# Routing each image by itself inside the causal attention, and POOL's selections of the last image ahead of its scatters

## What is computed

```python
t = t + _L3_attn_ref(_ln_t(t), L3_attn_w_qkv, L3_attn_w_out)   # causal attention, 8 heads of 16, per image
t = t + _L3_ffn_ref(_ln_t(t), W_router, W1, b1, W2, b2)        # 8 experts, top 2
# inside _L3_ffn_ref:
logits = x_flat @ W_router
topk_p, topk_i = jax.lax.top_k(softmax(logits), 2)
```

## Time and profile before

| | us |
|---|---|
| median of 3 runs | 1439.09 (1438.96 to 1439.64) |
| the profiled execution's own time | 1437.34 |
| its span, first to last instruction | 1435.5 |
| busy in the span: PE, DVE, ACT, POOL | 1106.5, 844.0, 676.1, 609.9 |

### The profile page before, as it was taken

How to read it: one execution, slowest core, us unless ns; L and a number is a source line. 1 busy time by engine, 2 the same in 40 slices (tenths; PEclk the granted TensorE clock), 3 DMA queues, 4 the chain that set the end, 5 groups by cost and what they waited for, 6 DMA issues and landing times. The chain is left out here.

```text
span 1435.5 us, 31817 instructions
## 1 busy us (share of the span) xinstructions
PE 1106.5 (77%) x9500; PEld 890.7 (62%) x9500; DVE 844.0 (59%) x2747; ACT 676.1 (47%) x1475; POOL 609.9 (42%) x873
## 2 busy tenths in 40 slices
PE   4549785888797967393799999548999984489982
PEld 3339553455465756262699999525667663489981
DVE  5754697663658754652355555356565574567764
ACT  3422473563555544161466666315555641355541
POOL 4600243035655533177134444212246667466660
PEclk9859998999999966597799999859999995699995
DMA  2148001100000005311111111124000001222216
GB/s 73 49 78 120 7 29 40 24 13 13 9 11 1 3 2 240 135 54 52 34 49 48 48 48 46 45 77 163 1 10 24 20 20 41 55 61 59 62 55 178
DMA packets 83095, 75.11 MB, mean 52 GB/s; under 512 B 21808, under 2 KB 75824, under 8 KB 81712
## 3 DMA queue, kind: packets, MB, share of 16 engines
q1 hardware_dynamic: 72880, 53.01, 13.4%
q0 software_dynamic: 9984, 20.53, 4.4%
q10 hardware_dynamic: 128, 0.26, 0.1%
HBM read 44.82 MB, written 29.48 MB: 52 GB/s over the span
## 5 line engine op out<-in xcount | busy, mean ns | idle before, releaser
L1782 POOL DMA_INDIRECT ys_scratch<-m_yout,m_xin x152 | 161.3, 1061 | 208.8 <-DVE m_yout L1884 147.8
L1816 PE MATMUL m_eps_up<-m_ext,m_w_up 128*128 128x128 f32 x1856 | 237.5, 279 | 0.7 <-DVE m_w_up L1863 0.7
L1816 PEld LDWEIGHTS m_eps_up<-m_ext,m_w_up 128*128 128x128 f32 x1856 | 222.5, 194 | 2.9 <-issue 1.2
L1826 PE MATMUL m_eps_y<-m_w_down,m_ht 128*128 128x128 f32 x1216 | 160.5, 275 | 0.6 <-DVE m_ht L1876 0.5
L1826 PEld LDWEIGHTS m_eps_y<-m_w_down,m_ht 128*128 128x128 f32 x1216 | 147.8, 192 | 1.0 <-DVE m_ht L1876 0.7
L1837 ACT ACTIVATE m_w_up<-m_up 128x512 f32 x152 | 95.8, 630 | 102.3 <-PE m_eps_up L1816 48.3
L1297 POOL TENSOR_TENSOR a_z<-a_y,a_peak 128x16 f32<-128x16 f32 (+31 forms) x64 | 67.6, 1057 | 105.7 <-DVE a_peak L1208 94.1
L2326 DVE TENSOR_REDUCE c_peak<-c_ps_s 128x2 f32<-128x256 f32 (+1 forms) x128 | 65.3, 552 | 80.4 <-PE c_ps_s L2617 79.9
L1840 ACT ACTIVATE m_w_down<-m_down 128x512 f32 x152 | 94.4, 621 | 17.4 <-PE m_eps_y L1826 17.2
L2165 POOL TENSOR_SCALAR_AFFINE_SELECT c_e<-c_e 128x256 f32<-128x256 f32 x128 | 49.2, 409 | 123.2 <-ACT c_e L2242 123.1
L1201 DVE SCALAR_TENSOR_TENSOR a_y<-a_y,a_ps_row 128x1 f32<-128x1 f32 (+51 forms) x256 | 72.3, 282 | 38.7 <-POOL a_z L1297 29.5
(11 more groups left out here) (394 smaller groups left out, 2595.2 us busy)
## 6 DMA issues: line engine op xcount, KB each, us to landing
m_xin<-xs_scratch SPq DMA_DIRECT2D x152, 64.5 KB, 1.8
xs_scratch<-empty SPq DMA_DIRECT2D x12, 516.0 KB, 11.0
m_y<-ys_scratch SPq DMA_DIRECT2D x22, 256.0 KB, 5.0
m_up<-in_m_gate SPq DMA_DIRECT2D x2, 2048.0 KB, 7.5
m_up<-in_m_up SPq DMA_DIRECT2D x2, 2048.0 KB, 11.9
m_down<-in_m_down SPq DMA_DIRECT2D x2, 2048.0 KB, 23.7
a_q_in<-q_scratch SPq DMA_DIRECT2D x80, 32.0 KB, 1.7
c_rows<-ys_scratch SPq DMA_DIRECT2D x10, 256.0 KB, 3.6
```

Of the source, the lines that this page charges most:

```text
L1782: pool.indirect_dma_start(ys_dram, bass.IndirectOffsetOnAxis(xin[:, u, C:C + 1].bitcast(U32), 0), yout[:, u, :], None).then_inc(stored[u], 16)
L1816: last = pe.matmul(ps[u % 2][:, k * P:(k + 1) * P], w[:, u % 2, k * P:(k + 1) * P], xt[:, u % 2, :], start=True, stop=True)
L1826: last = pe.matmul(ps_y[u % 2][:, 0:C], ht[:, u % 2, k, :], w_down[:, u % 4, k, :], start=(k == 0), stop=(k == KC - 1))
```

## The change

All lots hold one image. There are 16 passes of choosing and ranking in place of 11, one at every step. `send(b)` is at step `b+6` for every image. At step `B` = 16, POOL runs all the selections of image 15, also that of quarter 3 which stood at step 17, ahead of `invert(13)` and of the scatters; before, four scatters stood ahead of the selection of quarter 2 and four more ahead of that of quarter 3.

```diff
-LAST_PAIR = 10
-LOTS = [(b, 2) for b in range(0, LAST_PAIR, 2)] + [(b, 1) for b in range(LAST_PAIR, B)]
+LOTS = [(b, 1) for b in range(B)]
...
             for i in range(-2, B + 7):
                 before, last_but_one = 0 <= i - 1 < B, 0 <= i - 2 < B
-                if last_but_one:
+                if last_but_one and i <= B:
                     cut_off(i - 2, 3)
                 if before:
                     cut_off(i - 1, 0)
-                if before:
                     cut_off(i - 1, 1)
+                if i == B:
+                    cut_off(i - 1, 2)
+                    cut_off(i - 1, 3)
                 if 0 <= i - 3 < B:
                     invert(i - 3)
-                if 0 <= i - 7 < LAST_PAIR:
-                    send(i - 7, 0, 2)
-                if LAST_PAIR <= i - 6 < B:
+                if 0 <= i - 6 < B:
                     send(i - 6, 0, 2)
-                if before:
+                if before and i < B:
                     cut_off(i - 1, 2)
-                if 0 <= i - 7 < LAST_PAIR:
-                    send(i - 7, 2, 4)
-                if LAST_PAIR <= i - 6 < B:
+                if 0 <= i - 6 < B:
                     send(i - 6, 2, 4)
                 if 0 <= i - 4 < B:
                     copy_rows(i - 4)
```

## The result

| us | before | changed |
|---|---|---|
| median of 20 runs each | 1440.61 (1436.63 to 1442.78) | 1448.85 (1440.90 to 1456.76) |
| ratio, 95% interval | | 1.0052 (1.0039 to 1.0066) |
| the profiled execution's own time | 1437.34 | 1450.59 |
| its span | 1435.5 | 1448.9 |

The change is slower, by 0.5% in the ratio and 8.2 us between the medians. 1441.0 had been forecast and 1444.5 was the top of the range. The changed kernel's runs also lie wider apart: 16 us against 6.

What follows compares the result with a forecast made beforehand. DVE's path between row maxima, plus 7.6 us set by PE, was taken to bound each step. Steps +9.0 and end -7.1 gave +1.9 us, 1441.0 us on the median; range 1438.5 to 1444.5.

Steps and rivals of the forecast that it cites:

- what bounds a step: Steps of the attention: DVE's path from first to third row maximum, plus a constant 7.6 us set by PE.
- Rival 3: Steps 6 to 15: DVE hides the extra choosing passes, path 6.15 us; faster, 1432.5 us; chance 0.07.
- the way: DVE, first to third maximum in steps 6 to 15: 7.00 us each, +9.0 us in total.
- The upper end of 10.0: Top of the steps' cost: 0.1 us more at each of ten steps for PE's wait for the logits.
- the wait for the logits: PE waits for the logits ahead of the rank; 0.1 us more per step, only in the upper end.
- the end: From step 16 to the last padding: earlier selection of quarter 3 lets the padding land 7.1 us earlier.
- the other is 0.5 us: Step 16, clock already halved when the last quarter is weighed: gain 6.6 us instead of 7.1.
- a gain of 5.7 as its lower bound: Block's end: gain is only 5.7 us if POOL's scatters, not the padding, end it.
- the added wait: Step 16: DVE waits in shift_of(13) for invert(13), delaying PE's rank and weighing; weighing 6.6 us earlier, not 8.8.
- Rival 1: Last scatter groups: POOL bounds the end, 0.5 us more per group of four; slower, 1443.3 us; chance 0.17.
- its own sign: Block's end: padding issued well before the last scatter would show POOL as the bound; forecast had the scatter 0.7 us ahead.
- Rival 2: Steps: choosing on DVE loses 0.39 us per step to POOL's selections; slower, 1444.9 us; chance 0.08.

Runs made afterwards that it cites:

- before_2: The kernel before the change, nothing changed, profiled a second time in one run; 1440.39 us.
- e9: Changed kernel with fifteen idle bf16 matmuls of 384 columns at three places of PE's step 16; median 1448.99 us, ratio 1.0071 to before.
- e1_again: Second profile of the changed kernel with POOL's old order back, so only the routing image by image is left; one run, 1452.72 us.
- e1: Changed kernel with POOL's old order back, so only the routing image by image is left; median 1448.38 us, ratio 1.0070 to before.
- e5: Changed kernel with invert(13) moved between POOL's selections of quarters 2 and 3 at step 16; median 1448.13 us, ratio 1.0053 to before.
- e2: Kernel before, pairs kept, only POOL's selections of the last image moved ahead of all scatters of step 16; median 1439.85 us, ratio 1.0017.

## Why the prediction was wrong, point by point

**Right: what bounds a step.** The third maximum has no idle time, the second waits for PE, choosing and slots both stand between, and a step is its way plus 7.6 us. Rival 3 (hidden) did not occur as long as the order stayed. The lengths 14.7 to 14.8 fit the 14.6 that were named.

**A term mis-sized: the way.** It was put at 7.00 us and is 7.18. Of this 0.08 is the rank, 0.66 us for the 0.58 worked out from the earlier trace rows: of its three groups of matmuls the first takes 0.21 until the next starts, and 0.10 had been extrapolated for each added pair. The other 0.10 is the slots: they take 1107.88 - 1106.73 = 1.15 us, hardly less than the 1.21 of two images in the earlier trace rows; the 1.06 of the earlier trace rows stood at another step. The way is paid in ten steps, which makes 1.8 us; step 5 grew by 0.07, and the last 0.2 are spread over steps that were 0.01 to 0.03 longer. So 9.0 became 11.1. The upper end of 10.0 had only the wait for the logits in it.

**The step that failed: the end.** 7.1 us were forecast and 0.7 measured in the profiled execution, 2.4 when executions with the same early fall are compared. The prediction took the last exponential's place behind the maximum from the earlier trace rows as fixed, and weighed the clock only behind it ("the other is 0.5 us"), since it had fallen at 1189 in the one profile at hand. before_2, the same kernel, shows the exponential 4.8 us later. So the first term of the end's sum, the time from which POOL can select, had a spread of 4.8 us that one profile can't show. Before, eight scatters hid it; the change removes the scatters and makes the exponential the start of the chain. The gain counted from it, 8.8 us of which 6.6 were left, belongs to an execution with a late fall, and every profile of the changed kernel has an early one. With an early fall the exponential in before_2 is over at 1191.15 and the selection starts at 1196.77, so only 5.6 us were to be had, of which the weighing got 26.5 - 23.9 = 2.6 and the padding 2.4.

A smaller part of the miss has nothing to do with the exponential's place. The forecast has the padding 30.8 us behind the exponential's end (1223.56 - 7.1 - 1185.65), and it starts 32.4 behind it in all four profiles of the changed kernel. Of these 1.6 us, 0.8 are the rank matmuls at half the clock. The place of the last scatter was right: 34.8 behind the exponential's end by the forecast's 1220.4, 34.9 measured. So 7.1 - 1.6 - 4.8 gives the 0.7 that were measured, and a changed kernel with a late fall would have gained 5.5 us. That is an estimate from these figures, and e9, the changed kernel with idle matmuls and a late fall, bears it out: padding 32.4 and last scatter 34.9 behind the end of its last exponential. The prediction had kept a gain of 5.7 as its lower bound, for the case that POOL's scatters end the block, but went by the padding.

A second error stands beside it: the placement and the single lots were priced as one. The weighing was seen as freed from eight scatters, but the single lots had already taken four of them away. With an early fall, POOL issues the four that remain while it would wait for exponentials anyway, and the added wait and the four scatters put behind the last selection cost more than the placement saves (e1_again). With a late fall the two orders come out nearly even: the loads are 46.2 us behind the last exponential's start in e1's first profile and 45.6 in e9.

**Right: the added wait.** `shift_of(13)`, the logits' copy, `rank_of(11)`, the weighing: this chain stands in the profile word for word. The weighing is 3.8 us behind the exponential's end, for 3.0: the rank matmuls took 1207.31 - 1205.96 = 1.35 us at half the clock and not 0.58.

**Rival 1, POOL.** By its own sign, a last scatter behind the padding, it did not occur: the last scatter starts 2.1 us ahead of the end of SP's padding issue, as it did before, and not 0.7. Its price, 0.5 us more for each group of four, did not come either, since the last scatter is where the forecast had it. But the sign was badly chosen. The loads follow the last scatter wherever the two part (e5 above all), and POOL's queue is full from the last selection on but for the 0.39 us, so POOL was the bound of this end or as good as level with it.

**Rival 2, the port.** It did not occur, for its condition was hardly met. The choosing runs from 1108.56 to the third maximum at 1109.56, and POOL's selections beside it from 1106.76 to 1107.53 and again from 1109.40, so only the choosing's last instruction touches one. The second part of the way was 0.10 us longer than forecast, not 0.39. What the whole choosing would lose beside a selection, no run here shows. What does meet a selection is the slots' L2426, with two SBUF inputs: 0.62 us for its pair in the rows above, beside the first of these selections. At the end of the attention in e2, with POOL at scatters, DVE shows for the same pair:

```profile
1209.80 0.38 DVE L2431 TENSOR_TENSOR n_part<-n_rank,n_pick 128x16 f32<-128x16 f32 x2
```
By the Trainium skill, page "SBUF — State Buffer", section "Who interferes with whom", a DVE instruction with two SBUF inputs and a GpSimd instruction that reads SBUF exclude each other for the whole instruction. The trace's 0.62 against 0.38 agrees in sign; the price of a meeting was 0.24 us for two instructions, less than one selection's 0.39.

**The chances.** 0.30 was given to slower. The cases that made it up were POOL and the port, and neither happened as described; the cases that did, a clock that falls ahead of the last exponentials and a placement that costs more than it saves once eight scatters are four, had no chance of their own.

## What to carry over

Two edits that clear the same queue must be priced one behind the other, since the second finds only what the first left. A gain that consists in removing a queue in front of a late event has to be counted from the latest that the event can be, not from where one profile shows it: what the queue hid is free only as long as it stands. And profile the kernel before a second time ahead of explaining a difference: one more profile of it settled here what the experiments ahead of it had left open, whether the early fall is the change's doing. A sign that is to tell which of two engines ends a block must be one that parts them; in the one profile at hand the last scatter and the padding stood side by side, and either could have been it.
